# Third layer of a four-layer graph network: a second buffer for the normed rows, the norm at the head of VectorE's group, and the fourth feed-forward tile queued behind the next segments

## What is computed

```python
q = (h @ Wq); k = (h @ Wk); v = (h @ Wv)            # 8 heads of 64
e = einsum('ehd,ehd->eh', k[src], q[dst]) / 8       # one number per edge and head
attn = segment softmax of e over the edges of one target
a = segment_sum(attn * v[src], dst)
x = layernorm(h + a @ Wo, ln1_g, ln1_b)
f = relu(x @ W1 + b1) @ W2 + b2                     # hidden width 32
out = layernorm(x + f, ln2_g, ln2_b)
```

## Time and profile before

| | us |
|---|---|
| median of 3 runs | 3079.97 |
| lowest, highest | 3079.9, 3083.72 |
| the profiled execution, its own time | 3075.2 |
| its span, first to last instruction | 3073.4 |
| TensorE busy | 2371.3 (77%) |
| VectorE busy | 1852.2 (60%) |
| ScalarE busy | 1326.1 (43%) |
| first half of the third layer, from the first transpose to the last score copied out | 2065.8 to 2406.9 |
| second half, segment sums to the last norm | 2491 to 2695 |

### The profile page before, as it was taken

One profiled execution on the slowest core, in us unless ns is written; L12 is line 12 of the kernel. 1 busy time (PEld: TensorE's weight loads), 2 busy tenths in 40 slices (PEclk: granted clock), 3 DMA queues, 4 the chain that ended last, 5 costly groups with the idle time before them and its releaser, 6 DMA issues.

```text
span 3073.4 us, 29956 instructions
## 1 busy us (share of the span) xinstructions
PE 2371.3 (77%) x9660; PEld 1252.1 (41%) x9660; DVE 1852.2 (60%) x3783; ACT 1326.1 (43%) x1975; POOL 1132.5 (37%) x829
## 2 busy tenths in 40 slices
PE   5779999999999547989155667618888788668877
PEld 2445555555555323545021112114444655235455
DVE  3379889898898850235744434352554646827753
ACT  2898888888874321121132323201111113255544
POOL 1363544536457614330525555610120020043322
PEclk8899999999999768999568888858888688679989
DMA  7223333333433135334634555660120020132212
GB/s 202 81 63 117 106 107 103 105 112 93 120 101 89 45 93 140 95 82 144 195 117 129 155 159 160 149 182 18 41 58 23 28 53 27 54 90 68 74 46 54
DMA packets 212761, 297.93 MB, mean 97 GB/s; under 512 B 98581, under 2 KB 98951, under 8 KB 211258
## 3 DMA queue, kind: packets, MB, share of 16 engines
q1 hardware_dynamic: 107696, 213.63, 23.3%
q0 software_dynamic: 104960, 82.99, 10.7%
HBM read 171.39 MB, written 160.48 MB: 108 GB/s over the span
## 4 chain that ended last, share of the span: by engine, by line
PE 42%; DVE 21%; issue 11%; ACT 10%; POOL 8%; DMA 6%; SPq 2%; DVEq 0%; POOLq 0%; ACTq 0%
PE bank L1792 10%; PE bank L849 5%; POOL arena L1428 5%; POOL arena L941 4%; ACT RD L416 3%; PE bank L2339 3%; PE bank L829 3%; DVE st L527 3%; PE bank L291 2%; DMA arena<-y_table,ids 2%; PE bank L292 2%; PE bank L2222 2%; DVE lst L887 2%; ACT arena L469 1%; PE bank L276 1%
## 5 line engine op out<-in xcount | busy, mean ns | idle before, releaser
L941 POOL DMA_INDIRECT arena<-x_table,idd x120 | 151.5, 1263 | 752.4 <-DVE arena L1999 188.6
L284 PE MATMUL bank<-arena 128*125 128x512 f32 x640 | 290.0, 607 | 41.3 <-DMA arena<-x_cols 23.9
L1792 PE MATMUL bank<-arena 128*125 128x512 f32 x640 | 299.7, 626 | 0.7 <-ACT arena L857 0.7
L1428 POOL DMA_INDIRECT arena<-y_table,ids x180 | 229.7, 1276 | 153.0 <-DMA y_table<-arena 100.9
L857 ACT ACTIVATE arena<-bank 128x500 f32<-128x500 f32 (+1 forms) x210 | 115.2, 589 | 383.5 <-PE bank L829 252.5
L1477 PE MATMUL bank<-arena 125*125 125x512 f32 x360 | 205.4, 702 | 96.9 <-DMA arena<-y_table,ids 94.1
L300 PE MATMUL bank<-arena 128*125 128x512 f32 x640 | 278.6, 593 | 1.3 <-ACT arena L393 1.3
L661 POOL TENSOR_TENSOR arena<-arena,rowv 125x512 f32<-125x512 f32 x80 | 106.9, 1371 | 461.3 <-PE bank L292 167.7
L1637 DVE SCALAR_TENSOR_TENSOR arena<-arena,v,bank 125x512 f32<-125x512 f32 x180 | 134.5, 747 | 205.0 <-PE bank L1477 192.3
L1529 ACT ACTIVATE bank<-arena 125x512 f32<-125x512 f32 x180 | 107.9, 601 | 272.8 <-DVE arena L1637 263.0
L849 PE MATMUL bank<-arena 128*125 128x512 f32 x480 | 210.3, 596 | 8.0 <-DVE arena L1347 8.0
(11 more groups left out here) (392 smaller groups left out, 4891.5 us busy)
## 6 DMA issues: line engine op xcount, KB each, us to landing
y_table<-arena SPq DMA_DIRECT2D x36, 896.0 KB
p_table<-arena SPq DMA_DIRECT2D x25, 896.0 KB
z_table<-arena SPq DMA_DIRECT2D x25, 896.0 KB
x_table<-arena SPq DMA_DIRECT2D x25, 896.0 KB
arena<-x_cols SPq DMA_DIRECT2D x20, 1000.0 KB, 6.1
arena<-x SPq DMA_DIRECT2D x20, 896.0 KB
out<-arena SPq DMA_DIRECT2D x20, 896.0 KB
x_by_src<-arena SPq DMA_DIRECT2D x5, 896.0 KB
```

The lines of the kernel that those rows point to most:

```text
L284: i = nc.tensor.matmul(b[0:P, :], xT[:, k, j * P:(j + 1) * P], W1r[:, k, :], start=k == 0, stop=k == KC - 1)
L941: nc.gpsimd.indirect_dma_start(out=dst, out_offset=None, in_=table, in_offset=bass.IndirectOffsetOnAxis(ap=idx, axis=0), bounds_check=limi ...
L1428: nc.gpsimd.indirect_dma_start(out=V1[0:P, t, :], out_offset=None, in_=Yd[i % 2], in_offset=bass.IndirectOffsetOnAxis(ap=ids[:, 2, t:t + 1 ...
L1792: i = nc.tensor.matmul(b[0:P, :], fT[:, k, j * P:(j + 1) * P], W[:, k, :], start=k == 0, stop=k == KC - 1)
```

## The change

Four edits in the third layer:

- `T2x = (T2, KQ2)`: the normed rows of group g go to `T2x[g % 2]`; all readers of `T2` in the first half follow.
- VectorE's norm of group g (`dve_ln`) moves from the end of its group g to the head of it, so one group of TensorE's work ahead of its reader. ScalarE's root for it moves to right behind the four target banks of group g, ahead of `hidden`.
- `KQ2` is no longer free for the key times query product, which is formed in the slot of `V2` that the value copy fills afterwards; so each tile is reduced to its scores at once, between product and value copy. The four reductions at the group's end go. The preparation of the last group's scores (`e_rdy`) comes behind `dve_ln_scale`.
- In the second half `pe_ffn_second` gets a `tiles` argument. Steps 2 to 5 issue tiles 0 to 2 only; the fourth tile is issued in the next step, behind its segment sums. Step 6 issues everything.

```diff
+        T2x = (T2, KQ2)
...
-        def pe_ffn_second(pe, c, done):
+        def pe_ffn_second(pe, c, done, tiles=(range(RN), range(RN, TG))):
             pe.wait_ge(T_sb, done)
-            for js in (range(RN), range(RN, TG)):
+            for js in tiles:
...
                     pe.wait_ge(L_y, y2_first(g - 1))
-                    pe_transpose_rows(pe, c, T2)
+                    pe_transpose_rows(pe, c, T2x[(g - 1) % 2])
...
                     summed[i_] = c.t
+                if i_ >= 3:
+                    pe_ffn_second(pe, c, hidden, (range(RN, TG),))
...
                 if before is not None:
-                    pe_ffn_second(pe, c, hidden)
+                    pe_ffn_second(pe, c, hidden, (range(RN),) + ((range(RN, TG),) if i_ == EG + 1 else ()))
...
                 if g < EG:
                     for k in range(KC):
                         act_evac(act, c, Y[:, k, :])
+                    act_root(act, c)
                 if g:
                     hidden(T)
                     act_root(act, c)
...
                     act_ln_rows(act, g - 1, U2, x3_rows, NB2)
-                if g < EG:
-                    act_root(act, c)
...
             def tile(g, j):
                 t = TG * g + j
-                dve_evac(dve, c, lambda b: nc.vector.tensor_copy(KQ2[:, j, :], b[0:P, :]))
+                dve_evac(dve, c, lambda b: nc.vector.tensor_copy(V2[:, t, :], b[0:P, :]))
                 dve.wait_ge(R_sb, c.r)
-                dve_evac(dve, c, lambda b: nc.vector.tensor_tensor(KQ2[:, j, :], KQ2[:, j, :], b[0:P, :], ALU.mult))
+                dve_evac(dve, c, lambda b: nc.vector.tensor_tensor(V2[:, t, :], V2[:, t, :], b[0:P, :], ALU.mult))
+                dve.wait_ge(R_sb, c.r)
+                link(dve, c, nc.vector.tensor_reduce(EE[:, t, :], V2[:, t, :].rearrange("p (h d) -> p h d", h=H), AX.X,
+                                                     ALU.add))
                 dve_evac(dve, c, lambda b: nc.vector.tensor_copy(V2[:, t, :], b[0:P, :]))

             for g in range(EG):
-                res = XS2[(g - 1) % 2]
+                res, Tn = XS2[(g - 1) % 2], T2x[(g - 1) % 2]
+                dve.wait_ge(*x2_s[g].full(16 * TG))
+                dve_ln(dve, c, XS2[g % 2], dst=T2x[g % 2])
...
                 tile(g, 3)
-                dve.wait_ge(R_sb, c.r)
-                for j in range(TG):
-                    i = nc.vector.tensor_reduce(EE[:, TG * g + j, :],
-                                                KQ2[:, j, :].rearrange("p (h d) -> p h d", h=H), AX.X, ALU.add)
-                link(dve, c, i)
-                if g == EG - 1:
-                    start = v20[:, 9, :]
-                    link(dve, c, nc.vector.tensor_scalar(start, RD[:, :, Q_DSC], float(FAR), NEG, ALU.is_lt, ALU.mult))
-                    nc.vector.tensor_copy(EN[:, :, :], b3(start, H)).then_inc(e_rdy, 1)
                 if g:
                     dve_ln_scale(dve, c)
-                dve.wait_ge(*x2_s[g].full(16 * TG))
-                dve_ln(dve, c, XS2[g % 2], dst=T2)
+                dve.wait_ge(R_sb, c.r)
+            start = v20[:, 9, :]
+            link(dve, c, nc.vector.tensor_scalar(start, RD[:, :, Q_DSC], float(FAR), NEG, ALU.is_lt, ALU.mult))
+            nc.vector.tensor_copy(EN[:, :, :], b3(start, H)).then_inc(e_rdy, 1)
```

More of the change, by code:

```diff
@@ L1993, in dve_L2 @@
                         dve.wait_ge(x3_put, 32 * (g - 1))
-                    ffn_in(T2, U2)
+                    ffn_in(Tn, U2)
                 tile(g, 0)
@@ L1998, in dve_L2 @@
                     dve_ln_root(dve, c, U2)
-                    nc.vector.tensor_tensor(T2, res, spread(row(R_LN2B), TG), ALU.add).then_inc(shifted, 1)
+                    nc.vector.tensor_tensor(Tn, res, spread(row(R_LN2B), TG), ALU.add).then_inc(shifted, 1)
                 tile(g, 1)
                 if g:
-                    tail_scale(U2, T2, False)
+                    tail_scale(U2, Tn, False)
                 tile(g, 2)
@@ L2005, in dve_L2 @@
                     dve.wait_ge(shifted, g)
-                    tail_sum(U2, T2)
+                    tail_sum(U2, Tn)
                 tile(g, 3)
-                dve.wait_ge(R_sb, c.r)
-                for j in range(TG):
-                    i = nc.vector.tensor_reduce(EE[:, TG * g + j, :],
-                                                KQ2[:, j, :].rearrange("p (h d) -> p h d", h=H), AX.X, ALU.add)
-                link(dve, c, i)
-                if g == EG - 1:
-                    start = v20[:, 9, :]
-                    link(dve, c, nc.vector.tensor_scalar(start, RD[:, :, Q_DSC], float(FAR), NEG, ALU.is_lt, ALU.mult))
-                    nc.vector.tensor_copy(EN[:, :, :], b3(start, H)).then_inc(e_rdy, 1)
                 if g:
                     dve_ln_scale(dve, c)
-                dve.wait_ge(*x2_s[g].full(16 * TG))
-                dve_ln(dve, c, XS2[g % 2], dst=T2)
+                dve.wait_ge(R_sb, c.r)
+            start = v20[:, 9, :]
+            link(dve, c, nc.vector.tensor_scalar(start, RD[:, :, Q_DSC], float(FAR), NEG, ALU.is_lt, ALU.mult))
+            nc.vector.tensor_copy(EN[:, :, :], b3(start, H)).then_inc(e_rdy, 1)
             last_U, last_res = U2, XS2[(EG - 1) % 2]
```

## The result

The changed kernel took 3026.73 us (median of 4 runs, 3020.86 to 3036.18); the kernel before 3079.93 in the same comparison. The ratio is 0.9827, 95% interval 0.9803 to 0.9851: 1.7% faster, 53.2 us. The forecast was 3038.6 with a range of 3029 to 3052, so the direction held and the size was short: 41.4 us forecast, 53.2 measured, 2.3 us beyond the range. In a second comparison the same kernel took 3029.87 (6 runs, 3019.9 to 3046.68), ratio 0.9838 (0.9802 to 0.9874), 49 us less than the 3079.2 of the kernel before beside it, and 0.9 us inside the range. So the miss is small; what makes it worth following is that one part of the gain wasn't in the sum at all.

A forecast was written before the change was run, and what follows sets the result against it. TensorE's products were taken as the bound, left at group boundaries for the norm and, in the second half, alternating with VectorE. Gains 9.7 + 17.4 + 6.5 + 7.8 = 41.4 us from 3079.97 gave 3038.6, range 3029 to 3052.

The forecast's parts named there:

- first to last value copy: First half, groups 1 to 4, between the first and last value copy of a group: gain put at 0.
- (a): Rival: the clock gives nothing back, the second half little; 31.5 us less, feed-forward stretches slower, 3058 us; chance 0.10.
- (b): Rival: TensorE's clock stays high over the shrunk gaps; 50 us less and feed-forward stretches gain too, 3025 us; chance 0.07.
- the end of the first half: After the last group: reductions no longer precede score preparation, TensorE fills ten banks earlier; gain 6 to 7.5, taken as 6.5 us.
- step 2 to 3: Second half: segment sums move into TensorE's 4.17 us wait ahead of the fourth tile; gain 3.8 to 6.4, taken as 5 us.
- the boundaries: Between first-half groups: gap 0/1 closes, gain 9.7 us; the other three shrink to 3.0 us, gain 17.4 us together.
- the 61 to 64 us named as a sign: Sign that the forecast is right: first-half groups take 61 to 64 us.
- (c): Rival: ScalarE's moved root ahead of `hidden` is late, 1 us per us of slip at boundary 0/1; 3040 us, within forecast's 0.76.
- (d): Rival: the store wait at `ffn_in` in groups 2 to 4 becomes TensorE's bound; 3090 us at 27 us; chance 0.02.
- (e): Rival: the norm is moved but three boundary gaps stay, as ScalarE's part ends no earlier; 3056 us; chance 0.03.
- steps 3 to 5: Second half: step 3 to 4 gains only VectorE's idle time, 2.8 us; step 4 to 5 nothing.
- VectorE's first residual of step 4: Sign that the forecast is right: in the second half this residual comes without idle time, where VectorE idled 2.85 us.

The follow-up runs named there:

- the fill: Kernel before plus eight throwaway matmuls in each of the four big gaps at the group boundaries: 3065.04 us, ratio 0.9952.
- The fill: Kernel before plus one throwaway matmul ahead of the three feed-forward tiles and one ahead of the fourth, first half's four groups: 3061.39 us, ratio 0.9935.
- the fourth tile alone: Kernel before with only the second half's fourth feed-forward tile moved behind the next segment sums: four executions, 3056.11, 3067.72, 3233.77 and 4586.15 us, no ratio.

## Why the prediction was right and where it was short

**The step that failed** is a term that the sum put at nothing: it left first to last value copy at the 43.1 us a group of before, and let the clock there move only in rivals (a) and (b). The four groups took 7.4 us less in the first profile and 3.2 in the second. Two smaller terms were under-sized: the end of the first half (6.5, measured 8.9) and step 2 to 3 (5, measured 8.8 and 6.2). The rest of the table comes to nothing in the first profile and to 2 us less gain in the second. In all the stretch gave 13.5 us more than the 41.4 forecast in one execution and 4.7 in the other.

**Right, the boundaries.** The gap of 7.39 us shrank to 2.95 (forecast 3.0), ended by ScalarE's emptying of the banks, and vanished at the first boundary. All four together gave 26.3 us in the first profile (24.9 + 75.4 less 15.0 + 59.1, with rounding) and 26.2 between the second ones, where 9.7 + 17.4 = 27.1 stood. Runs with one edit each and the fill bear out both parts of this price: the gap of 4.96 us without the reductions, and 2.6 us of slow clock behind a gap. The groups themselves came shorter than the 61 to 64 us named as a sign, 59.6, 61.4, 59.7 in the first profile, which is the failed term again. The reductions in the tile cost nothing visible, VectorE's wait for the value bank fell from 2.68 to 2.02. The moved root and the moved `ffn_in` held nobody up, so rivals (c) and (d) didn't occur; (e) didn't either, since the gaps went from 7.4 to 2.95; the wait for the store is 3.39 us and is still hidden.

**Right, steps 3 to 5.** 2.7 and 3.0 us for a forecast of 2.8; here VectorE is the bound and the store's wait remains (2.55 us ahead of the feed-forward input). VectorE's first residual of step 4 starts without idle time, as said. Step 4 to 5, put at nothing, gave 0.5 and 0.9.

**Short, the term that was not there.** First to last value copy summed to 170.8 us before and to 163.4 and 167.6 after. The loss had been in the trace: the fourth tile at half rate, and the products behind it at 0.52, in each group of before. The steps of the sum asked where an engine waits, and this loss is no wait. The fill shows that it is rate: held at the 2.4 GHz level the same code takes 38.6 a group. What it doesn't show is that the change is what gave the 7.4 and 3.2 back. The unedited first half in the run with the fourth tile alone summed to 162.9, and the changed kernel with its gaps filled to 169.1, so this term moves as much without the change as with it. So a part of the 53 us may be luck.

**Short, the end of the first half.** 8.9 us instead of 6.5 in both profiles. The forecast took the copies at 0.71 us each and the transposes in part at the slow pace. The ten copies took 5.94 us, 0.59 each, where one that stands alone shows as 0.67, and TensorE, after a wait of only 1.50 us, did ten banks in 5.45.

**Short, step 2 to 3.** 8.8 and 6.2 us instead of 5. The term stood between 3.8, with the segments at the slow clock, and 6.4 at the fast. They ran at full rate in one execution (3.84 us) and at 0.61 in the other (6.01). The upper bound was mis-worked: with edge features, segments and fourth tile at the full rate (1.3, 3.6 and 2.0 us in the changed kernel or rows 8, from 2547.93 on) the tile ends at 2554.8, before VectorE's `ffn_in` does (2555.56 in the trace of before), so with add and statistics, 3.8 us, VectorE is free at 2559.4 and not at 2561.5. That makes 8.5, and 8.8 was measured. In the other execution the segments were slow, but the fourth tile behind them ran at the full rate (1.12 and 1.02 us, where the lower bound had 3.7 for both), hence 6.2 and not 3.8.

**The range.** Its upper end of the gain was 50 us, from the terms' own bounds, and left the spread of the medians on that side out, though rival (b) stood at 3025. The two comparisons gave 53 and 49. By stretches the change is worth 46 to 55 us in this layer. Three small slips in the sums change nothing of this: rows 3 give 3.60 - 1.87 = 1.7 us for slow transposes behind a gap, not 1.9; rival (a) adds 5 for the end of the first half, whose own lower bound is 6; and the 11.2 of rival (b) is 6.4 + 4.8 only if the store gets faster, which it didn't: step 3 to 4 gave 2.7 and 3.0.

**Open.** What decides between the two outcomes of the same code, 43.1 or 40.1 us in the groups of before, 41.6 or 43.0 after, wasn't settled. Of three executions of the unedited first half, two went at 68.3 us a group and one, that of the fourth tile alone and so of another program, at 64.5. That shorter gaps keep the clock high at the tiles, theory A's second claim, is not shown: filling the gaps of before went with a sum of 164.8 for 170.8, filling those of the changed kernel with 169.1 for 163.4 and 167.6. With two profiles of each kernel and one of the others, a frequency can't be given. Nor was it tried to shift the layer's start on purpose.

## What to carry to other kernels

Moving a step off TensorE's path by one stage is worth the gap that it leaves minus what then ends the wait; look for the second-latest releaser in its own engine's order, which here left 3 of 7.4 us. Price a gap at its idle time plus the half-rate work behind it, and look for half-rate stretches also where no long wait stands, around short waits with small matmuls: two throwaway matmuls a group there gave 18 us, as much as a third of this change. When two versions differ by a per cent or less, compare stretches between landmarks, and take a second profile of each before explaining anything.

## What the runs showed of the hardware

The granted clock of one stretch of one program is not the same in each execution: 32 segment records of the changed kernel took 3.84 us at 1.00 in one profile and 6.01 at 0.61 in the other. At the fourth tile of the first half it was 0.50 in two profiles of the kernel before and 1.00 in another program with the same code there, with the same 0.74 us wait ahead, worth 3 us a group. Behind waits of 0.88 and 0.74 us, with narrow matmuls between them, the products ran for 6.2 us at 0.52; with a matmul in each wait they ran at 1.00, and all four groups were 4.5 us shorter. A gap of 7.39 us cost 2.6 us of slow clock behind it, which eight matmuls in the gap gave back. Transposes alone also ran at the full rate, 32 in 3.58 us without a product between. And the time at which the code ahead of the layer is through differed by 11 us between two executions of one program, and by 22 over all runs, of 3000.
